# Whole fp32 products instead of three split ones in a three-layer graph network, with part of the shifts on VectorE and the third layer's bias on TensorE

## What is computed

```python
def _sage_conv(h, src, dst, Wl, bl, Wr):
    msg = h[src]
    s = jax.ops.segment_sum(msg, dst, num_segments=N_NODES)
    cnt = jax.ops.segment_sum(jnp.ones((src.shape[0], 1), h.dtype), dst, num_segments=N_NODES)
    agg = s / jnp.maximum(cnt, 1.0)
    return agg @ Wl.T + bl + h @ Wr.T
...
for Wl, bl, Wr, g, b in params:
    h = residual + _sage_conv(h, src, dst, Wl, bl, Wr)
    h = _layer_norm(h, g, b)
    h = _prelu(h, a_prelu)
    residual = h
...
x = _layernorm(x + h)
```

## Time and profile before

| | us |
|---|---|
| median of three runs | 2077.23 |
| the profiled execution | 2078.05 |
| its span, first to last instruction | 2076.2 |
| TensorE busy in it | 1991.9 |

### The profile page before, as it was taken

The page is one execution under the profiler, slowest core; times in us unless marked ns, Lnnn a source line. Parts: engine busy times, 40 slices in busy tenths (PEclk is TensorE's granted clock), DMA queues, the critical chain, the costliest instruction groups (busy, mean ns, idle before and its releaser), DMA issues. The chain is left out here.

```text
span 2076.2 us, 30403 instructions
## 1 busy us (share of the span) xinstructions
PE 1991.9 (96%) x10149; PEld 1653.8 (80%) x10149; DVE 1539.4 (74%) x2382; ACT 1206.4 (58%) x2643; POOL 1513.0 (73%) x1122
## 2 busy tenths in 40 slices
PE   6999999999999999999999999999899999999992
PEld 4777888788888888888888888887778888888882
DVE  6556676667567655666666666669999999999994
ACT  3774455445444455544444444458877777777774
POOL 2788888888888766655555555558878888888886
PEclk8999999999999999999999999999999999999996
DMA  5566676566666654544444444455666666666652
GB/s 182 180 209 231 201 233 213 193 223 205 207 210 206 188 160 174 173 150 149 150 150 148 149 152 153 142 168 198 220 213 209 211 213 209 203 207 208 200 190 89
DMA packets 181073, 387.66 MB, mean 187 GB/s; under 512 B 20117, under 2 KB 20562, under 8 KB 180918
## 3 DMA queue, kind: packets, MB, share of 16 engines
q1 hardware_dynamic: 142358, 272.06, 38.9%
q0 software_dynamic: 38560, 113.67, 17.2%
HBM read 221.07 MB, written 164.79 MB: 186 GB/s over the span
## 5 line engine op out<-in xcount | busy, mean ns | idle before, releaser
L393 PE MATMUL ps_z<-w_hi,hT_hi 128*128 128x512 f32 x1884 | 764.1, 406 | 11.1 <-ACT ps_z L519 10.5
L662 POOL TENSOR_TENSOR y<-y,shift 128x1024 f32<-128x1024 f32 (+1 forms) x237 | 614.4, 2592 | 172.2 <-DVE y L767 169.4
L393 PE MATMUL ps_z<-w_hi,hT_lo 128*128 128x512 f32 x1884 | 739.9, 393 | 0.0
L393 PE MATMUL ps_z<-w_lo,hT_hi 128*128 128x512 f32 x1884 | 739.1, 392 | 0.0
L519 ACT COPY ps_z<-bias_rows 128x512 f32<-128x512 f32 x471 | 276.4, 587 | 459.6 <-DVE y L767 402.5
L755 DVE TENSOR_TENSOR hT_lo<-ps_t,hT_hi 128x1024 fp32r<-128x1024 f32 (+1 forms) x237 | 287.5, 1213 | 328.9 <-ACT hT_hi L490 328.3
L393 PEld LDWEIGHTS ps_z<-w_hi,hT_hi 128*128 128x128 f32 x1884 | 355.4, 189 | 83.3 <-issue 16.1
L393 PEld LDWEIGHTS ps_z<-w_hi,hT_lo 128*128 128x128 f32 x1884 | 354.2, 188 | 79.4
L499 ACT ACTIVATE junk<-ps_z 128x512 f32<-128x512 f32 x471 | 277.5, 590 | 229.2 <-PE ps_z L393 223.7
L393 PEld LDWEIGHTS ps_z<-w_lo,hT_hi 128*128 128x128 f32 x1884 | 355.6, 189 | 67.3
L767 DVE SCALAR_TENSOR_TENSOR y<-ps_z,rstd,gain 128x512 f32<-128x512 f32 x471 | 330.2, 742 | 57.0 <-POOL rstd L650 57.0
(11 more groups left out here) (131 smaller groups left out, 1974.4 us busy)
## 6 DMA issues: line engine op xcount, KB each, us to landing
h_scratch<-hout SPq DMA_DIRECT2D x156, 512.0 KB
hin<-h_scratch SPq DMA_DIRECT2D x156, 512.0 KB, 3.8
x_by_slot<-hin SPq DMA_DIRECT2D x78, 512.0 KB
o_sb<-x_by_slot SPq DMA_DIRECT2D x78, 512.0 KB
rowtab<-edge_row_table SPq DMA_DIRECT2D x60, 256.0 KB
stage<-in_WrT SPq DMA_DIRECT2D x3, 1024.0 KB
stage<-in_WlT SPq DMA_DIRECT2D x3, 1024.0 KB
hin<-in_x,node_get POOLq DMA_INDIRECT x157
```

The lines of the kernel that those rows point to most:

```text
L393: mm = pe.matmul(acc, a[:, k, :], ww[:, k, :], start=False, skip_group_check=True, stop=stop and k == KC - 1 and a is a_lo)
L662: nc.gpsimd.tensor_tensor(y[u.r2][:, 0:u.n, :], y[u.r2][:, 0:u.n, :], moved, ALU.add).then_inc(shifted, 1)
```

## The change

There is one weight tile `w_sb` in fp32 for each product, one `hT` for each unit and `sumT` as it is, with no high and low parts. `mm3` becomes `product`: one fp32 matmul for each chunk where there were three fp32r matmuls. `take_low`, `take_sum_high`, `take_sum_low` and `split_weight` are gone, and `take_high` is a plain copy, `take`. The shift is added by VectorE (`add_shift_here`) for all units of the first layer and the units at even places of the third, 119 in all, and by GpSimd for the others. In the third layer `fill` does nothing: TensorE begins each bank with an fp32 matmul of `first_row` (ones in the first row, else nought) and the bias rows, and waits for `gained` itself.

```diff
+    def here(no):
+
+        l, pos = divmod(no, UL)
+        return l == 0 or l == L - 1 and pos % 2 == 0
...
-                reach(pe, low, u.no)
+                reach(pe, taken, u.no)
...
-            def mm3(acc, a_hi, a_lo, w, stop):
+            def product(acc, a, w, stop):
 
                 for k in range(KC):
-                    for a, ww in ((a_hi, w_hi[w]), (a_hi, w_lo[w]), (a_lo, w_hi[w])):
-                        mm = pe.matmul(acc, a[:, k, :], ww[:, k, :], start=False, skip_group_check=True,
-                                       stop=stop and k == KC - 1 and a is a_lo)
+                    mm = pe.matmul(acc, a[:, k, :], w_sb[w][:, k, :], start=False, skip_group_check=True,
+                                   stop=stop and k == KC - 1)
                 return mm
...
-                pe.wait_ge(filled, u.ahead + j + 1)
-                mm = mm3(ps_z[u.r2][:, j, :], hT_hi[u.r2][:, j], hT_lo[u.r2][:, j], 2 * u.l, not u.edge)
+                if u.l < L - 1:
+                    pe.wait_ge(filled, u.ahead + j + 1)
+                else:
+                    before = Unit(u.no - 2)
+                    pe.wait_ge(gained, min(before.ahead + j + 1, before.upto))
+                    pe.matmul(ps_z[u.r2][:, j, :], first_row[:], bias_rows[:, u.l, :], start=True, stop=True)
+                mm = product(ps_z[u.r2][:, j, :], hT[u.r2][:, j], 2 * u.l, not u.edge)
...
-                nc.scalar.copy(hT_hi[u.r2][:, 0:u.n].rearrange("p j k n -> p (j k n)"),
-                               ps_t[:, 0:u.n, :].rearrange("p j d -> p (j d)")).then_inc(high, 1)
+                nc.scalar.copy(hT[u.r2][:, 0:u.n].rearrange("p j k n -> p (j k n)"),
+                               ps_t[:, 0:u.n, :].rearrange("p j d -> p (j d)")).then_inc(taken, 1)
...
-                if j >= u.n:
+                if j >= u.n or u.l == L - 1:
                     return
...
-            def take_low(u):
-                dve.wait_ge(high, u.no + 1)
-                nc.vector.tensor_tensor(hT_lo[u.r2][:, 0:u.n].rearrange("p j k n -> p (j k n)"),
-                                        ps_t[:, 0:u.n, :].rearrange("p j d -> p (j d)"),
-                                        hT_hi[u.r2][:, 0:u.n].rearrange("p j k n -> p (j k n)").bitcast(F32),
-                                        ALU.subtract).then_inc(low, 1)
...
+            def add_shift_here(u):
+                if not u.here:
+                    return
+                dve.wait_ge(gained, u.upto)
+                moved = shift[:, u.l:u.l + 1, :].to_broadcast([P, u.n, D])
+                nc.vector.tensor_tensor(y[u.r2][:, 0:u.n, :], y[u.r2][:, 0:u.n, :], moved, ALU.add).then_inc(shifted_here, 1)
```

More of the change, by code:

```diff
@@ L68, in __init__ @@
             self.r2, self.r3 = no % 2, no % 3
+            self.here = here(no)
+            self.shifts = len([n for n in range(no + 1) if here(n) == self.here])
             self.eno = len(edge_units) * self.l + self.tiles[0] // 2
@@ L112, in build_program @@
         hin = [sb(f"hin{i}", [P, 2, D]) for i in range(3)]
-        hT_hi = [sb(f"hT_hi{i}", [P, 2, KC, P], F32R) for i in range(2)]
-        hT_lo = [sb(f"hT_lo{i}", [P, 2, KC, P], F32R) for i in range(2)]
+        hT = [sb(f"hT{i}", [P, 2, KC, P]) for i in range(2)]
         y = [sb(f"y{i}", [P, 2, D]) for i in range(2)]
@@ L186, in build_program @@
         for w in range(2):
-            w_hi[w], w_lo[w] = sb(f"w_hi{w}", wide, F32R, early), sb(f"w_lo{w}", wide, F32R, early)
+            w_sb[w] = sb(f"w{w}", wide, where=early)
         early.close()
@@ L240, in build_program @@
         h_stored = [sem(f"h_stored{i}") for i in range(3)]
[L241 removed]
+        turned, taken, z_ready = sem("turned"), sem("taken"), sem("z_ready")
         squared, veps_done, rstd_done = sem("squared"), sem("veps_done"), sem("rstd_done")
[L243 removed]
+        gained, shifted, shifted_here, h_done, affine_signed = (
+            sem("gained"), sem("shifted"), sem("shifted_here"), sem("h_done"), sem("affine_signed"))
         rt_in = sem("rt_in")
         m_in = [sem(f"m_in{j}") for j in range(2)]
[L246 to L247 removed]
+        e_same, e_summed, e_carry = sem("e_same"), sem("e_summed"), sem("e_carry")
         xr_in = [sem(f"xr_in{i}") for i in range(OB)]
@@ L412, in product_mean @@
                 if u.tiles[0] == 0 and j == 0:
-                    pe.wait_ge(w_low, KC * (2 * u.l + 2))
-                pe.wait_ge(e_low, 2 * u.eno + j + 1)
-                mm3(ps_z[u.r2][:, j, :], sT_hi[j], sT_lo[j], 2 * u.l + 1, True).then_inc(z_ready, 1)
+                    pe.wait_ge(w_moved, KC * (2 * u.l + 2))
+                pe.wait_ge(e_carry, 2 * u.eno + j + 1)
+                product(ps_z[u.r2][:, j, :], sumT[j], 2 * u.l + 1, True).then_inc(z_ready, 1)
             def turn_table(parts):
@@ L477, in center @@
                 act.wait_ge(w_mean, KC * w + c + 1)
-                nc.scalar.activation(w_hi[w][:, c, :], stage[:, c, :], ACT.Identity,
-                                     bias=w_neg[:, c:c + 1]).then_inc(w_high, 1)
+                nc.scalar.activation(w_sb[w][:, c, :], stage[:, c, :], ACT.Identity,
+                                     bias=w_neg[:, c:c + 1]).then_inc(w_moved, 1)
             def center_bias(l):
@@ L519, in fill @@
                 nc.scalar.copy(ps_z[u.r2][:, j, :], bias_rows[:, u.l, :]).then_inc(filled, 1)
[L521 to L528, removed]
             def sign_tile(t):
@@ L569, in scalar_program @@
                 if ahead.exists:
-                    take_high(ahead)
+                    take(ahead)
                 old = Unit(T - 4)
@@ L657, in add_shift @@
             def add_shift(u):
-                if u.no == 0:
+                if u.here:
+                    return
+                if u.shifts == 1:
                     pool.wait_ge(affine_signed, 1)
@@ L806, in carry @@
                 dve.wait_ge(e_summed, 2 * u.eno + j + 1)
+                if u.eno > 0:
+                    before = Unit(EDGE_AT[u.eno - 1])
+                    dve.wait_ge(z_ready, before.ahead + j + 1)
                 if u.tiles[j] == 0:
@@ L817, in carry @@
                 ins.then_inc(e_carry, 1)
[L819 to L823, removed]
             def out_sum(u):
@@ L934, in vector_program @@
                     normal(last)
+                    add_shift_here(last)
                 if Unit(T + 3).exists:
```

44 lines of the change are left out of this document (15 added, 29 removed).

## The result

The changed kernel takes 2552.73 us (median of four runs, 2552.46 to 2553.39) against 2077.61 us before, 1.2287 times as long (95% interval 1.2266 to 1.2308). 2564 was forecast, in 2535 to 2680.

A forecast was written before the change was run, and what follows sets the result against it. TensorE's row of matmuls was taken as the bound: 2076.2 + 94.1 + 140.1 + 254.1 (layers) - 2 (tail) = 2562.5 us span, +1.85 outside, less 0.8 to the median: 2564 us, range 2535 to 2680.

The forecast's parts named there:

- What bounds the kernel: Whole kernel: a row of matmuls on TensorE; in the second layer they sum to 641.6 of 643.3 us.
- The price of a chunk: Product matmuls: two fp32 records at two cycles a column, 430 ns each (ends 427 and 454), 0.860 us a chunk.
- the rival with fp32r's extra: Product matmuls: each fp32 record also costs fp32r's extra 14 to 20 ns; 2620 to 2650 us, or 2685; chance 13%.
- The layers: TensorE by layer: 793.3, 783.4 and 919.7 us, which is +94.1, +140.1 and +254.1.
- The start: First layer: the second turn's 4.51 us wait for `hT_lo` shrinks by 4.5 us, needing ScalarE's copy alone.
- The drain: Tail after the last matmul, 36.2 us before: -2 us, ends -8 and +3.
- The wait for `gained`: Third layer's bias matmul waits for `gained` instead of the fill: price 0, end +10 us.
- The rival that a wait shows: Third layer: `gained` or VectorE's shifts hold TensorE by 1 us a unit, +79, 2640 us; chance 2%.
- The shift on VectorE: First and third layers: 119 shifts of 1.2 to 2.6 us each on VectorE, hidden behind TensorE, price 0.
- The fast rival: Product matmuls: one cycle a column at 512 columns, 0.455 us a chunk, 1650 us in all; chance 10%.
- The low clock of the earlier trace: Early bf16 157-column and fp32 40-column matmuls ran at 1.2 instead of 2.4 GHz; used to read cycles a column.

The follow-up runs named there:

- The two kernels that take one part back: Against the changed kernel: third-layer bias filled by ScalarE again, 2418.31 us; all shifts on GpSimd again, 2553.82 us.
- The 256-column kernel: The changed kernel with each 512-column product matmul issued as two of 256 columns, bias matmuls left whole: 2565.03 us.
- the kernel that pays it: The changed kernel with fp32r tiles and the same fp32r matmul issued twice per chunk, low parts left out: 1710.82 us.

## Why the prediction was right, point by point

- **What bounds the kernel.** It is a row of matmuls, and more so after the change than before. The two kernels that take one part back confirm it from both sides: 134.4 us for 314 records of the bias, nothing for 119 shifts.
- **The price of a chunk.** 0.860 forecast, 0.859 measured. The step that carried it was to count two records for each fp32 matmul, and to read two cycles a column from the end of the weight load to the end of the matmul. The 256-column kernel shows it as a price by columns. The choice of 430 ns between 427 and 454 was right: it was 429.3, and the rival with fp32r's extra is out. The reason given for it, that the transposes at the same half rate have 2 to 3 ns, was only half of one: bf16 matmuls have 2.4 ns at the full rate of one column a cycle, so it is not the half rate that spares a matmul the extra. The argument for that rival, that the extra is larger where DMA is busier, does not hold either, by the third layer above. The page "TensorE: Matmul & The Clock Gate" of the Trainium skill (section "Back-to-back issue gap") gives a single matmul 2.5 ns beside its columns. For fp32 that holds for each record (2.6 ns at 256 and at 512 columns), not for each of four passes, and it holds for bf16 (2.4 ns). For fp32r it does not hold (14 to 20 ns).
- **The layers.** Forecast 793.3, 783.4 and 919.7; measured 792.7, 780.7 and 914.9. The 0.7 ns a record make 3.5 of the 8.1 us too many; the rest are the 1.7 and 3 us of waits that I kept for the second and third layer and that went to nothing. The 6 us kept in the first layer came out in sum but not in kind: I had 2 for the low clock and 4 for waits. TensorE is idle in it for 1.3 us, and the granted clock over its first 15.4 us was 0.75, which costs an estimated 3.9 us.
- **The start.** Here a part was missed. I took the second turn's 4.5 us and left the first turn at its place; it came 2.2 us earlier (29.67 for 31.86), because VectorE's four low parts of the first weight (`w_lo`, 2.73 us from 24.28 us on) had stood before the row work that TensorE waits for. The last of that row work (L902 before, L893 now) ended at 31.08 us before and at 28.44 now; the first turn then waited 0.4 us for its rows. The sum has no term for it.
- **The drain.** 34.2 forecast, 33.1 measured.
- **The wait for `gained`.** Price 0, and it was 0: no wait of TensorE on the `y` of `normal` (L754) stands in the list (the `y` of L893 there is used before the loop). The rival that a wait shows is out too.
- **The shift on VectorE.** Hidden, as forecast, and 1.24 us each, at the lower end of 1.2 to 2.6. But I priced it only as work added, with GpSimd's 2.6 us as the upper end. I did not see that taking it from GpSimd gives VectorE back more than it costs, in shorter operations and in waits for `root`. This did not matter here, since VectorE was hidden anyway; in the kernel before, the same 119 shifts are worth 27.5 us and 158 of them 34.5.
- **The fast rival.** Its price was 1650 us; the kernel that pays it, with 0.454 us a chunk in the second layer and 0.468 in the first, takes 1711. Its bound was wrong as well: in the third layer it is TensorE with the bias, whose 135 us the sum for that rival had left out, and in the second the loop over the banks.

The sum of the differences is -2.2 at the start, -0.6, -2.7 and -4.8 in the layers and -1.1 in the drain, together -11.4: from 2562.5 to the span of 2551.1 us. All of them are small and of one sign; the total was near because the price of a chunk was within 0.2%, and the 2364 chunks make 2031 of the 2551 us.

**The low clock of the earlier trace rows.** The profile's granted clock reads 1.00 over those rows, so it does not show the low clock that the prediction puts there; the steps of the matmuls do:

```profile
9.16 0.34 PE L362 MATMUL ps_s<-sumT 128*128 128x157 bf16 x1
9.29 0.34 PE L360 MATMUL ps_s<-sumT,ones_short 128*128 128x157 bf16 x1
...
13.28 0.23 PE L361 MATMUL ps_s<-sumT 128*128 128x157 bf16 x1
13.35 0.23 PE L362 MATMUL ps_s<-sumT 128*128 128x157 bf16 x1
```

The step is 0.13 us for 157 columns, one each cycle at 1.2 GHz, and 0.07 from 13.2 us on, at 2.4. So the reading stands.

## What to carry to other kernels

Before replacing several reduced-precision matmuls by one whole fp32 matmul, price it in passes of the array, not in instructions: count its records in the trace, and find a small fp32 matmul from whose weight load to whose end the cycles a column can be read. Work moved off an engine that is never idle is worth its whole price (134.4 us here), and work moved between the others nothing (1.1 us). That holds only while it is never idle: the kernel before, whose TensorE was 96% busy, still gained 34.5 us from moving additions between two others. Before judging where an operation belongs, look at how much it stretches the neighbour's operations, and at what stands behind it in its own queue: the cheaper place was the engine that looked nearly full.

## What the runs showed of the hardware

- An fp32 matmul is two records, each at two array cycles a column: 429 ns for 512 columns, 216 for 256, 0.859 us for a 128x128x512 product, where three fp32r matmuls take 0.682 to 0.70.
- An fp32r matmul of 512 columns steps by 227 ns, by 234 in the first layer; bf16 by 216 in the same places. The amount that DMA moves explains neither: 227 ns stood beside both 153 and 205 GB/s.
- VectorE's fp32 operations with two operands in SBUF took 0.75 us (128x512) and 1.27 us (128x1024) with no addition of GpSimd beside them. In the third layer of the kernel before, a PReLU that began behind an addition took 3.07 us and ended 1.09 us behind it; where the PReLU began first it took 1.27 us and the addition 2.86 instead of 2.42. Operations with one of their two tensors in PSUM were not held up (0.34 and 1.22 us either way).
- After TensorE's waits of 2.89 and 3.34 us its granted clock fell to half for 3 to 6 us, and 512-column fp32r matmuls stepped by 0.43 us instead of 0.23.
